# Expert weights split during attention, and a reordered shared stage, in a cross-attention and expert kernel

## The reference

```
x = x + tanh(g_xattn[0]) * quantised_product(layernorm(x), ctx)
x = x + tanh(g_ffn[0])   * ternary_feed_forward(layernorm(x))
x = x + tanh(g_xattn[1]) * attention(layernorm(x), ctx, ctx, mask)
x = x + tanh(g_ffn[1])   * experts(layernorm(x))
```

```
expert e:  (silu(x @ gate_w[e]) * (x @ up_w[e])) @ down_w[e]        512 -> 352 -> 512
shared:    (silu(x @ s_gate_w + b) * (x @ s_up_w + b)) @ s_down_w + b   512 -> 704 -> 512
```

## Time and profile before

| | |
|---|---|
| time, median of 3 runs | 1141.89 us (1140.69 to 1152.41) |
| profiled execution, span | 1146.9 us; the time of this execution by itself is not recorded |
| busy in the span | PE 1028.8 (90%), DVE 747.0 (65%), ACT 601.8 (52%), POOL 456.0 (40%) |
| mean granted TensorE clock | 0.962 |
| DMA | 142.39 MB, mean 124 GB/s |

### The profile page before, as it was taken

The page is one execution under the profiler, slowest core; times in us unless marked ns, Lnnn a source line. Parts: engine busy times, 40 slices in busy tenths (PEclk is TensorE's granted clock), DMA queues, the critical chain, the costliest instruction groups (busy, mean ns, idle before and its releaser), DMA issues. The chain is left out here.

```text
span 1146.9 us, 17729 instructions
## 1 busy us (share of the span) xinstructions
PE 1028.8 (90%) x5438; PEld 475.5 (41%) x5439; DVE 747.0 (65%) x1419; ACT 601.8 (52%) x898; POOL 456.0 (40%) x483
## 2 busy tenths in 40 slices
PE   0466889999789999999999998999998899999996
PEld 0243445555423223323322324455445455555542
DVE  6988988888786776578477547745545344443347
ACT  6897999999346776467467565452211111111110
POOL 1100335544410242243134341000657788889065
PEclk9978899999979999999999999998999899999998
DMA  9322930000534234134211004201678888976588
GB/s 325 114 74 80 342 138 1 2 1 9 133 89 107 80 82 116 62 58 94 66 48 44 12 21 136 76 26 52 243 282 170 200 205 207 206 192 146 153 284 291
DMA packets 174204, 142.39 MB, mean 124 GB/s; under 512 B 121364, under 2 KB 137108, under 8 KB 173624
## 3 DMA queue, kind: packets, MB, share of 16 engines
q1 hardware_dynamic: 163560, 110.40, 34.7%
q0 software_dynamic: 8672, 29.76, 7.9%
q10 hardware_dynamic: 1904, 1.38, 0.6%
HBM read 70.93 MB, written 43.37 MB: 100 GB/s over the span
## 5 line engine op out<-in xcount | busy, mean ns | idle before, releaser
L1432 ACT ACTIVATE prob<-p_col,mask_col,any_key 128x512 f32<-128x512 f32 x256 | 186.2, 781 | 103.2 <-PE p_col L1564 102.3
L1653 DVE CUSTOM_DVE_ANT_0 ajunk<-p_row,mask_row 128x512 bf16<-128x512 f32 x256 | 166.2, 686 | 64.1 <-PE p_row L1513 62.5
L1526 PE MATMUL p_out<-prob,v 128*64 128x512 f32 x512 | 138.1, 618 | 0.1
L1332 POOL TENSOR_TENSOR o<-sum_a,rec 32x512 f32<-32x512 f32 x30 | 39.1, 1304 | 186.1 <-DMA rec<-inv_d 184.0
L1513 PE MATMUL p_row<-ks,early_place 99*128 99x512 f16 x256 | 100.5, 395 | 8.7 <-DVE top L1653 8.0
L1564 PE MATMUL p_col<-early_place,ks 101*128 101x512 f16 x256 | 97.7, 385 | 0.9 <-ACT prob L1432 0.3
L2647 DVE SCALAR_TENSOR_TENSOR shid<-s_up,ssilu 128x352 f32<-128x352 f32 x39 | 20.4, 524 | 99.0 <-PE s_up L2565 98.8
L2513 ACT ACTIVATE ssilu<-s_gate 128x352 f32<-128x352 f32 x39 | 18.1, 463 | 124.0 <-PE s_gate L2565 124.0
L2578 PE MATMUL s_down<-mw,shT 128*128 (+1 forms) x351 | 82.0, 379 | 0.0
L2565 PE MATMUL s_gate<-mw,sxT 128*128 x444 | 74.1, 318 | 6.7 <-DMA sxT<-x_slots 6.7
L2565 PE MATMUL s_up<-mw,sxT 128*128 x444 | 73.5, 316 | 0.0
(11 more groups left out here) (354 smaller groups left out, 2077.3 us busy)
## 6 DMA issues: line engine op xcount, KB each, us to landing
x_slots<-nought SPq DMA_DIRECT2D x3, 3328.0 KB, 18.4
y_slots<-y SPq DMA_DIRECT2D x39, 256.0 KB, 2.2
early_place<-in_ctx SPq DMA_DIRECT2D x8, 1024.0 KB, 6.2
early_place<-halves_d SPq DMA_DIRECT2D x45, 128.0 KB, 2.5
halves_d<-halves SPq DMA_DIRECT2D x18, 256.0 KB, 2.1
mstg<-in_L_ffn_gate_w POOLq DMA_DIRECT2D x6, 704.0 KB, 5.7
mstg<-in_L_ffn_up_w POOLq DMA_DIRECT2D x6, 704.0 KB, 6.0
x<-in_x SPq DMA_DIRECT2D x4, 1024.0 KB, 7.3
```

What stands on the lines that cost most here:

```text
L1432: nc.scalar.activation(prob[s % 4][:, c, :], p_col[c][:], ACT.Exp, bias=mask_col[:, b, k:k + 1], scale=any_key[:, b:b + 1]).then_inc(t_exp, 1)
L1526: mm = nc.tensor.matmul(p_out[pr][c * 2 * DH:(c + 1) * 2 * DH, :], v1[b % 2][:, k, g, :], prob[n % 4][:, c, :], start=(k == 0), stop=(k == ...
L1653: nc.vector.tensor_tensor_reduce(junk[:, n % 2, :], p_row[n % 2][:], mask_row[:, blk // HPG, :], 1.0, -3e38, ALU.add, ALU.max, top[blk % 2 ...
```

## The change

- In attention GpSimd also loads experts 2 to 7, part by part, into what was the staging area of the attention weights, splits each with two one-input instructions and a subtraction into one buffer of halves (`both`), and stores them to `split_d` in memory. `PARTS_AT` says how many parts follow the normalisation in each turn of its loop: 3, 3, 2, 2, 1, 2, 2, 2, 1, 2, 2, 2.
- In the shared stage the transposes of tiles 4 to 15 leave TensorE and ScalarE: SyncE issues them as DMA transposes (`turn_rows`) between the weight loads. The normalised rows have two buffers. The router stands inside `gate_up(1, 0)`, `number_slots` inside `gate_up(1, 1)`; VectorE's choice is cut in four pieces and moved forward; loads of experts 0 and 1 from the third part on move behind the stores of the shared weights. The scatters wait for given counts of products (`SCATTER_AFTER`). Four tiles instead of two are transposed ahead.
- In the tiles GpSimd issues one load per expert of both halves, two in flight, and splits nothing; `e_have` counts the experts that have come. The loads for the late shared expert are issued after 15 pairs of tiles instead of after 2.

Not shown: `xn` becomes a list of two, `choose` is cut into `probabilities`, `best_two`, `choose` and `shares` with the same instructions, `add` takes a range of tiles, and names are passed on.

```
@@ -79,6 +79,7 @@
+    split_d = nc.dram_tensor("split_d", (EXPERTS - EARLY, P, 2, WC), F16).ap()
     x_d = a["x"].rearrange("b (t p) d -> b p t d", p=P)
...
@@ -1340,11 +1344,48 @@
 
+            t_ew = (t_ew0, t_ew1)
+            parts = [(e, q) for e in range(EARLY, EXPERTS) for q in range(len(W_PARTS))]
+            stage = [wst[:, n * KB * EI:(n + 1) * KB * EI] for n in range(2)]
+            both = wst[:, 2 * KB * EI:3 * KB * EI].bitcast(F16).rearrange("p (h c) -> p h c", h=2)
+
+            def load_expert(c):
+                e, q = parts[c]
+                load_part(nc.gpsimd, stage, t_ew, q, *(a["L1_ffn_" + t][e] for t in ("gate_w", "up_w", "down_w")))
+
+            def split_expert(c):
+
+                e, q = parts[c]
+                at, n, _ = W_PARTS[q]
+                w32 = stage[q % 2][:, 0:n]
+                pool.wait_ge(t_ew[q % 2], 16 * (c // 2 + 1))
+                need(pool, t_ed, 16 * c)
+                pool.nop(nofuse=True)
+                nc.gpsimd.tensor_scalar(both[:, 0, 0:n], w32, W_UP, 0.0, ALU.mult, ALU.add).then_inc(t_eh, 1)
+                nc.gpsimd.tensor_scalar(w32, w32, W_UP, 0.0, ALU.mult, ALU.add).then_inc(t_es, 1)
+                pool.wait_ge(t_eh, c + 1)
+                pool.wait_ge(t_es, c + 1)
+                pool.nop(nofuse=True)
+                nc.gpsimd.tensor_tensor(both[:, 1, 0:n], w32, both[:, 0, 0:n], ALU.subtract).then_inc(t_el, 1)
+                pool.wait_ge(t_el, c + 1)
+                pool.nop(nofuse=True)
+                nc.gpsimd.dma_start(split_d[e - EARLY, :, :, at:at + n], both[:, :, 0:n]).then_inc(t_ed, 16)
+                if c + 2 < len(parts):
+                    load_expert(c + 2)
+
+            pool.wait_ge(t_split, KB + 1)
+            load_expert(0)
+            load_expert(1)
+            done_parts = 0
             for blk in range(BLOCKS + 1):
                 if blk > 1:
                     normalise(blk - 2)
                 if blk % HPG == HPG - 1 and blk < BLOCKS - 1:
                     ln_power(blk // HPG + 2)
+                for c in range(done_parts, done_parts + PARTS_AT[blk]):
+                    split_expert(c)
+                done_parts += PARTS_AT[blk]
+            pool.wait_ge(t_ed, 16 * len(parts))
             for done in spent:
                 pool.sem_clear(done)
...
@@ -1136,6 +1138,8 @@
+    PARTS_AT = (3, 3, 2, 2, 1, 2, 2, 2, 1, 2, 2, 2, 0, 0, 0, 0, 0)
...
+SCATTER_AFTER = [("up", n) for n in (11, 12)] + [("down", n) for n in (10, 12)] + [("up", n) for n in (13, 13, 14, 14, 15)] + \
+    [("down", n) for n in (13, 14, 15, 16)] + [("up", n) for n in (16, 17, 17)]
+FIRST = 4
...
@@ -1954,19 +1999,39 @@
-            for u, q in ORDER:
-                weights(u, q)
+            def turn_rows(*tiles_):
+                for t in tiles_:
+                    b = t // TPB
+                    if t % TPB == 0:
+                        sp.wait_ge(m_xl, b)
+                    sp.dma_start_transpose(xT[:, :, :, t * P:(t + 1) * P].rearrange("p h k s -> p (h k) s"), row_of(t)).then_inc(m_turned[b - 1], 16)
+
+            weights(1, 0)
+            weights(1, 1)
+            turn_rows(4, 5)
+            weights(0, 2)
+            turn_rows(6)
+            weights(0, 3)
+            turn_rows(7)
+            weights(1, 2)
+            turn_rows(8, 9)
+            weights(1, 3)
+            turn_rows(10, 11, 12, 13, 14, 15)
+            weights(2, 0)
+            weights(2, 1)
...
+            for u, q in ORDER[8:]:
+                weights(u, q)
...
-            for n in range(2):
+            for n in range(FIRST):
...
@@ -1990,8 +2055,12 @@
+            pace = {2 * k: after for k, after in enumerate(SCATTER_AFTER)}
             for t in range(NT):
                 for s in range(2):
+                    if 2 * t + s in pace:
+                        done, count = pace[2 * t + s]
+                        pool.wait_ge({"up": m_up, "down": m_down}[done], count)
                     nc.gpsimd.indirect_dma_start(out=x_slots, out_offset=bass.IndirectOffsetOnAxis(ap=dest[:, s, t:t + 1], axis=0),
                                                  in_=row_of(t), in_offset=None).then_inc(m_scat, 16)
...
@@ -2052,23 +2121,20 @@
-            hidden(0, 0, lambda: high(1), lambda: high_parts(1, 0, 1), lambda: high_parts(0, 2, 3))
+            def high_next():
+                high_parts(1, 0, 1)
+                high(2)
+
+            hidden(0, 0, lambda: high(1), high_next, lambda: high_parts(0, 2, 3))
...
-            turned(4)
-            turned(5)
-            high(2)
-            hidden(0, 1, lambda: high_parts(1, 2, 3))
-            for t in range(6, 10):
-                turned(t)
-            high(3)
+            hidden(0, 1, lambda: None, lambda: None, lambda: high(3))
+            high_parts(1, 2, 3)
...
-            for t in range(10, NT):
-                turned(t)
             act.wait_ge(m_shift, 1)
             nc.scalar.activation(logit[:], logit[:], ACT.Exp).then_inc(m_exp, 1)
-            hidden(1, 1, lambda: high_part(2, 2), lambda: high_part(2, 3))
+            hidden(1, 1, lambda: None, lambda: high_part(2, 2), lambda: high_part(2, 3))
...
@@ -2095,7 +2160,8 @@
                                           start=False, stop=(s == NT))
                 mm.then_inc(m_before, 1)
 
-            def gate_up(g, n):
+            def gate_up(g, n, *between):
                 if n == 0:
...
@@ -2155,19 +2221,12 @@
             turn_router()
-            turn(4, 5)
             gate_up(0, 1)
-            turn(6, 7)
             down(0, 0)
-            turn(8, 9)
-            gate_up(1, 0)
-            turn(10, 11)
-            down(0, 1, 12, 13)
-            turn(14, 15)
-            router()
-            gate_up(1, 1)
+            gate_up(1, 0, lambda: None, router)
+            down(0, 1)
+            gate_up(1, 1, number_slots)
             down(1, 0)
-            number_slots()
             gate_up(2, 0)
...
@@ -2206,21 +2265,23 @@
             statistics(1)
-            for n in range(2):
-                for h in range(2):
-                    low_piece(n, h)
+            low_piece(0, 0)
+            low_piece(0, 1)
             normalise(1)
+            low_piece(1, 0)
+            low_piece(1, 1)
+            statistics(2)
...
@@ -2299,25 +2369,36 @@
-            hidden(0, 0, lambda: low_rows(1), lambda: low_parts(1, 0, 1), lambda: low_parts(0, 2, 3))
+            def first_rows():
+                low_rows(1)
+                normalise(2)
+
+            def second_rows():
+                low_rows(2)
+                dve.wait_ge(m_b, 16)
+                nc.vector.tensor_scalar(bias_dg[:], bias_dg[:], gates[:, 3:4], None, ALU.mult)
+
+            def third_rows():
+                statistics(3)
+                normalise(3)
+
+            hidden(0, 0, first_rows, lambda: low_parts(1, 0, 1), lambda: low_parts(0, 2, 3))
...
-            statistics(2)
-            normalise(2)
-            dve.wait_ge(m_b, 16)
-            nc.vector.tensor_scalar(bias_dg[:], bias_dg[:], gates[:, 3:4], None, ALU.mult)
-            low_rows(2)
-            hidden(0, 1, lambda: low_parts(1, 2, 3), lambda: statistics(3))
-            add(0, 0)
-            normalise(3)
+            hidden(0, 1, second_rows, third_rows)
+            add(0, 0, 0, 2)
             low_rows(3)
-            hidden(1, 0, lambda: low_part(2, 0), lambda: low_part(2, 1))
-            add(0, 1)
+            add(0, 0, 2, TPB)
+            low_parts(1, 2, 3)
+            hidden(1, 0, lambda: low_part(2, 0), lambda: low_part(2, 1), probabilities)
+            best_two()
+            add(0, 1, 0, 2)
             choose()
-            hidden(1, 1, lambda: low_part(2, 2), lambda: low_part(2, 3))
+            add(0, 1, 2, TPB)
+            shares()
+            hidden(1, 1, find_slots, lambda: low_part(2, 2), lambda: low_part(2, 3))
             add(1, 0)
-            find_slots()
             hidden(2, 0, lambda: low_part(3, 0), lambda: low_part(3, 1))
...
@@ -2422,15 +2503,16 @@
+            with sp.Fori(FIRST // 2, PAIRS_OF_TILES - 1) as r:
                 for n in range(2):
                     body(r, n)
             for n in range(2):
                 body(PAIRS_OF_TILES - 1, n, n == 0)
 
-            sp.wait_ge(m_wl, NQ * (2 + EXPERTS) + MORE)
+            sp.wait_ge(e_have, EXPERTS)
...
@@ -2451,45 +2533,19 @@
-            nc.gpsimd.memset(up256[:], W_UP).then_inc(e_pool, 1)
...
-            def split(e, more):
...
-                    nc.gpsimd.tensor_tensor(half(e, 0, q), s, up256[0:r].broadcast_to([r, n]), ALU.mult).then_inc(m_wh, 1)
-                    nc.gpsimd.tensor_scalar(s, s, W_UP, 0.0, ALU.mult, ALU.add).then_inc(e_pool, 1)
...
-                    nc.gpsimd.tensor_tensor(half(e, 1, q), s, half(e, 0, q), ALU.subtract).then_inc(m_wl, 1)
...
-            load(EARLY, 0)
-            load(EARLY, 1)
-            with pool.Fori(EARLY, EXPERTS - 1) as e:
-                split(e, True)
-            split(EXPERTS - 1, False)
+            for e in range(EARLY):
```

(16 more changed lines are left out.)

108 lines of the change are left out of this document (46 added, 62 removed).

## The result

The changed kernel takes 1236.37 us (median of 3 runs, 1234.95 to 1240.09) against 1141.89: a ratio of 1.078 (95% interval 1.073 to 1.083). The forecast was 1163, the range 1133 to 1184: the sign was right, the size four and a half times too small (21 us against 94). The profiled spans are 1238.0 and 1146.9 us.

A forecast was written before the change was run, and what follows sets the result against it. TensorE was taken as the bound, nearly full in attention, shared stage and tiles. Span 1146.9 + 34.7 (attention) - 7 (shared stage) - 6 (tiles) = 1168.6, less 5.0 gives 1163 us; range 1133 to 1184.

The forecast's parts named there:

- Which stage pays for what: Whole kernel: gains only from TensorE's gaps (13 us), losses from whatever makes a full TensorE wait (34.7 us in attention).
- GpSimd's walk in attention: Attention: split parts and store waits delay GpSimd's normalisations block by block, 34.7 us lost, ends 6 and 45.
- the 3.65 by which I had 8 us less: Attention: the Trainium skill's landing time for a 704 KB GpSimd DMA; with it the walk loses about 26 us.
- all 13.9 us of block 0: Attention: six parts delay block 0's normalisation, so ScalarE's copy of block 2 comes 13.9 us late and TensorE waits.
- my own sign, a gap under 5 us: Attention: a TensorE gap near 394 under 5 us would mean the forecast is wrong and the change gains.
- VectorE: nothing on the path, up to 5 more.: Attention: VectorE's subtractions stretch beside GpSimd's split, but its slack covers it: 0 us, otherwise up to 5 us more.
- The shared stage: Shared stage: transposes off TensorE and two waits removed, less one new wait before down's third result: gain 7 us, ends 2 and 11.
- The tiles, a gain of 6 us: Expert tiles: the 6.4 us wait for rows and slow products after it vanish; gain 6 us, ends minus 10 and 9.3.
- the rival's place and cause: Tiles: bulk loads starve row transposes, some eight tiles lack 3.4 us each, 27 us, total 1196; chance 0.12.
- the bytes are the same and lie in longer pieces: Tiles: argument against bulk loads starving the transposes, beside four tiles standing ready; that rival had chance 0.12.
- starved tiles: Tiles: rival that bulk loads hold up the row transposes, 33 us above the forecast, 1196; chance 0.12.
- a kernel that gets faster: Attention: rival that GpSimd stays within its slack and the change pays, 1127 to 1130; chance 0.18.

The follow-up runs named there:

- e1: The changed kernel with GpSimd's split of the six routed experts put back among the tiles: 1143.99 us, 0.997 of the kernel before.
- e2: The kernel before with only the split of six experts added to GpSimd in attention, its result unused: 1194.19 us, 1.038 of the kernel before.
- e8: The changed kernel with split parts spread evenly over attention's blocks, bulk loads paced by the tiles and cut into eight strips: 1195.23 us, 1.043 of before.
- e11: The kernel before plus the 24 parts' loads, stores and waits on GpSimd in attention, without their arithmetic: 1184.95 us, 1.030 of before.
- e15: The kernel before plus the 24 parts' arithmetic on GpSimd in attention, with two loads and no stores: 1158.37 us, 1.011 of before.
- e13: The changed kernel with all six bulk loads given to GpSimd's queue at once, full rows, at the tiles' start: 1207.48 us, 1.053 of before.
- e14: The changed kernel with all six bulk loads given to ScalarE's queue at once, full rows, at the tiles' start: 1206.97 us, 1.052 of before.
- e3: The changed kernel with each expert's bulk load cut into eight strips of 2176 B rows, all given at once: 1191.02 us, 1.036 of before.
- e5: The changed kernel with each expert's bulk load cut in two, rows of 8704 B, both given at once: 1222.07 us, 1.067 of before.
- e6: The changed kernel with full-row bulk loads one at a time, each begun when the one before has landed: 1189.06 us, 1.038 of before.

## Why the prediction was wrong

- **Which stage pays for what.** Right: a gain only from TensorE's gaps, a loss from what makes it wait. e1, which has only the gains, is 4 us shorter than before by its runs (interval 0 to 7), and by stages 9, where I had 13.
- **GpSimd's walk in attention.** Right for the moments it was read from (402.93 for 402.7, 408.61 for 408.3; the stores landed in 4.4 us for the assumed 4.5, and against the 3.65 by which I had 8 us less). (The six parts add up to 42.4 us, not 42.5, which changes nothing.) Wrong for what they cost, the first failed step. The walk charged GpSimd with all 13.9 us of block 0, and ScalarE waited for it for 4.84. By my own sign, a gap under 5 us, the forecast was wrong there, though the gain that the sign promised didn't come either. Over the stage TensorE's waits that lead back to it are 12.3 us, where I had 34.7. The whole loss, 44.7 (45.2 in e2), is near my 34.7 by luck: chains that I had at nothing fill it, VectorE, transposes beside GpSimd's traffic, and products at the lower clock after each gap. Take GpSimd's lateness away (e8, e11) and the reciprocals come 12 to 17 us late in its place, behind transposes in SyncE's queue that are slow (e11) or start late (e8).
- **"VectorE: nothing on the path, up to 5 more."** Wrong: 10.9 us with the arithmetic by itself in e15. Its average slack, 116 of 342 us, is no cover for an instruction that TensorE waits for at once. And I had counted only the wide subtractions of rows: the 15 casts and 15 subtractions of 128x16 grew most, by 14.2 us in all, the 16 wide ones of this stretch by 2.7.
- **The shared stage.** 4.9 us for 7. The wait in front of the third result of `down` came as foretold (2.2 us at 814); one like it before the second (2.3 us at 782) was missed, VectorE being at the rows' split and the adds in a new order; with it I had no such term.
- **The tiles, a gain of 6 us.** The failed step that puts the time out of the range: they lost 51.4. I named the rival's place and cause, transposes beside bulk loads, but priced it from one row, 10.94 us for a transpose beside GpSimd's old loads, as 3.4 us for each of eight tiles. The old loads had pauses between them. A stream without one doesn't lengthen a transpose by a factor, it holds it until the stream ends: 22 to 24 us for 13 MB at 420 GB/s (e13, e14). In the form that the change chose it is 59, with two loads still to come; why that form crawls is open. "Against: the bytes are the same and lie in longer pieces" was the wrong way round: in the same form shorter pieces made less of the wait (e3, e5). Without that stall (e6) the tiles last 220.0 us from their first product to the last row tile's gate product, before 219.5, and with the old split (e1) 216.2: of the 9.3 us 3.3 were there to gain at most, for the wait moves to the next late thing.
- **The chance.** 0.12 for starved tiles, and 0.18 for a kernel that gets faster. The traffic should have weighed more: 26 MB more in attention, beside 12 transposes of x and those of ctx.

## What to carry to other kernels

A DMA transpose is hundreds of small packets, here 768 of about 250 B. Next to bulk loads from GpSimd's or ScalarE's queue it went at the pace of the bulk packets until that queue paused, so give bulk loads one at a time, with the landing of one before the issue of the next, wherever a transpose is on the path. Work moved to an idle engine is free only if its ports and its DMA traffic are free too: run the arithmetic alone and the traffic alone before adding up queue times. And ask what the old place cost: here GpSimd's split among the tiles cost TensorE no wait in before, and one of 4.3 us in e1.
